# Cross-attention with 1500 keys on one core: two-chunk steps in layer 1, a third context buffer, and another order of scores, search, product and preparation on TensorE

## The chip, the cores and the metric

The kernel runs on one core of a Trainium2 chip. The metric is the device time of one execution in microseconds (us). Six engines matter here: TensorE (PE, with its weight loads PEld), VectorE (DVE), ScalarE (ACT), GpSimd (POOL), SyncE (SP, whose queue issues all DMAs of this part), and the 16 DMA engines behind that queue.

## The reference

Two decoder layers over 32 batch entries ("sequences" below) of 56 query tokens, width 128, with a context of 1500 keys each. Both layers attend to the same context, which is projected anew in each. Around them stand layer norms and two mixtures of experts, which the change leaves alone.

```python
x = x + tanh(g_xattn[0]) * diff_attention(layernorm(x), ctx)          # layer 0: 32 score heads of 4, 16 value heads of 8
x = x + tanh(g_ffn[0])   * experts0(layernorm(x))
x = x + tanh(g_xattn[1]) * masked_attention(layernorm(x), ctx, mask)  # layer 1: 16 heads of 8, mask True = hidden key
x = x + tanh(g_ffn[1])   * experts1(layernorm(x))
# attention, per sequence and head: softmax(q k^T * scale) v, with k = ctx Wk, v = ctx Wv
```

## The kernel before

`attend(T, L)` runs once for each layer, one sequence after another. The keys of a sequence are cut in 12 chunks of 125 (`NKT`, `KT`) and in 3 thirds of 500 (`TK`). One step handles one chunk.

What TensorE does in a step, with the lines of the profile:

- **scores** (L962, L968): keys times queries for the chunk, transposed, so that keys lie on partitions. Layer 0 has 1792 score columns, in two halves of 896, one for each of the two two-bank PSUM buffers `score_ps`; the parameter `place` is 0 for the first half of a step and 1 for the second. Layer 1 has 896 columns, so a step fills one buffer, and two matmuls with the mask (`mask_f`, L962) go ahead of the eight with the keys (L968). ScalarE turns each buffer into probabilities (`exps`, L1075).
- **search** (L937): the row maxima of a later sequence, found piece by piece. A piece is a matmul of 112 rows by 500 keys; VectorE reduces it (L1133 in layer 0, L1130 in layer 1, where it adds `mask_add` on the way). There are 48 pieces for a sequence in layer 0 and 24 in layer 1, issued in pairs. Three PSUM banks (`rooms`) take them in turn, so a piece waits until the piece three before it is reduced.
- **weigh**, the product (L984): probabilities of the step before times values (`vext`), accumulated in `acc_ps`. Each matmul in f32 shows as two in the trace.
- **preparation** (`use`, and `drain` on ScalarE or VectorE), placed by the table `where`: T turns the context (layer 0, L895), K and V make keys and values of a third (L904, L911), M turns the maxima (L916), F turns the output (L921) and A the normalised attention (L925). In layer 0 they use the score buffer that is free just then; in layer 1 they take a turn in the three `rooms`. `LEAD` says for which sequence: K for three ahead, V for two ahead, M for the next, F and A for the one before.

The order in a layer 0 step is: scores 0, pair 0, scores 1, first half of the product, pair 1, preparation, second half of the product. In layer 1 it is: scores, the pair, the product, preparation. The search runs five steps further ahead than the sequence (`AHEAD`): from step 7 on it works on the sequence two ahead.

What is waited for across engines, and the part of it that matters here:

- `scores` of place 0 in layer 0 waits until all exponentials of the steps before are done (`s_exp`, L953 to L955). In layer 1 it waits only for those up to the step before the last.
- Keys take a way through DRAM to be laid out anew: ScalarE drains K into `key_f`, GpSimd splits it in two halves (`split_keys`, L806, L808), SP stores both (`store_k`, L679) and reads them back with six DMAs into `kstack` (`fill_k`, L689). The first piece of a sequence waits for all six (`s_ks`).
- SP issues in order. One round of its loop is: `fill_k(n + 2)`, `load_q(n + 3)`, `next_mask(n + 3)`, `next_context(n + 4)`, `fill_m(n + 1)`, `store_k(n + 3)`. `fill_m` (L699) waits for the maxima that M has turned and VectorE has split (L1106, L1108).

## Time and profile before

| | us |
|---|---|
| median of 3 runs (2349.38 to 2350.72) | 2349.78 |
| the profiled execution | 2345.43 |
| its span, first to last instruction | 2343.1 |

| | TensorE | VectorE | ScalarE | GpSimd |
|---|---|---|---|---|
| busy us of the span | 2179.4 | 1677.4 | 1507.4 | 1278.7 |
| share | 93% | 72% | 64% | 55% |

Layer 0's attention fills the span from about 100 to 1225 us and layer 1's from about 1400 to 2165 us. Most sequences take the same time to within a few hundredths of a microsecond: 35.0 us in layer 0 and 22.3 us in layer 1. So a sequence can be read once and multiplied. A row of the timeline gives the start, the busy time, the engine and line, what is written and read, and the idle time ahead of it with what ended it. The start of the next row is what tells how long a group holds the engine, since matmuls overlap.

### The profile page before, as it was taken

Reading aid. Unit: us, or ns where it says so; the run is one execution under the profiler, and the core shown is the slowest. Engines: PE = TensorE matmul, PEld = TensorE weight load, DVE = VectorE, ACT = ScalarE, POOL = GpSimd, SP = SyncE. Lnnn points to the kernel's source line nnn. Section 1 sums busy time; section 2 is a strip of 40 time slices with the busy share of each in tenths; the row PEclk is TensorE's granted clock in tenths of the full one; section 3 lists DMA queues with packets and bytes.
Section 4 is the critical chain, followed back from the end, with each engine's and each line's share of the span. In section 5 each row is a group of like instructions: output and inputs, shape, how many; then the busy total and the mean of one; then the engine's idle time right before and its main releaser. Section 6 shows DMA issues by size and latency. Waiting matters only on the chain. (4 is left out here: it accounts for less than half of the span.)

```text
span 2343.1 us, 67447 instructions
## 1 busy us (share of the span) xinstructions
PE 2179.4 (93%) x27256; PEld 1297.5 (55%) x27256; DVE 1677.4 (72%) x3701; ACT 1507.4 (64%) x2133; POOL 1278.7 (55%) x1418
## 2 busy tenths in 40 slices
PE   3799999999999999999976967999999999999798
PEld 2255555555555555555535853666665666666576
DVE  3688888888888888888825455777776677775644
ACT  2177787787787787787773322677676667667322
POOL 5335555555655655655423445677776777772332
PEclk9599999999999999999997985999999999999799
DMA  3635344344344344344201018576665666661100
GB/s 102 130 75 117 89 100 115 89 103 114 88 103 113 94 100 111 97 98 110 48 2 64 24 35 158 126 143 148 137 140 128 136 137 138 146 124 36 55 1 16
DMA packets 95245, 227.82 MB, mean 97 GB/s; under 512 B 46308, under 2 KB 58852, under 8 KB 88292
## 3 DMA queue, kind: packets, MB, share of 16 engines
q1 hardware_dynamic: 94692, 223.67, 42.3%
q8 instruction: 210, 3.44, 0.7%
q14 instruction: 87, 0.71, 0.1%
q10 hardware_dynamic: 256, 0.00, 0.0%
HBM read 146.77 MB, written 76.48 MB: 95 GB/s over the span
## 5 line engine op out<-in xcount | busy, mean ns | idle before, releaser
L1075 ACT ACTIVATE probs<-score_ps 125x896 f32<-125x896 f32 x1152 | 1014.2, 915 | 203.3 <-PE score_ps L968 200.9
L1133 DVE TENSOR_REDUCE max_part<-max_ps 112x1 f32<-112x500 f32 x1024 | 654.3, 668 | 115.2 <-PE spare_ps L937 66.9
L984 PE MATMUL acc_ps<-probs,vext 125*32 125x224 f32 (+1 forms) x12288 | 670.7, 316 | 2.7 <-issue 2.1
L937 PE MATMUL max_ps<-kstack,qstack 48*112 48x500 f16 x1535 | 507.1, 405 | 4.7 <-DVE max_part L1133 2.6
L968 PE MATMUL score_ps<-qstack,kstack 50*125 50x224 f16 (+1 forms) x6144 | 453.6, 243 | 15.7 <-ACT probs L1075 13.9
L968 PEld LDWEIGHTS score_ps<-qstack,kstack 50*125 50x125 f16 x6144 | 343.1, 134 | 181.1 <-issue 120.2
L1130 DVE CUSTOM_DVE_ANT_0 kstack<-max_ps,kstack 112x500 f32<-112x500 f32 x511 | 335.2, 675 | 127.1 <-PE max_ps L937 75.0
L1133 DVE TENSOR_REDUCE max_part<-spare_ps 112x1 f32<-112x500 f32 x512 | 343.1, 670 | 64.3 <-PE max_ps L937 64.3
L984 PEld LDWEIGHTS acc_ps<-probs,vext 125*32 125x32 f32 x12288 | 260.8, 109 | 220.1 <-issue 151.0
L937 PE MATMUL spare_ps<-kstack,qstack 48*112 48x500 f16 x769 | 310.0, 403 | 19.2 <-issue 15.8
L937 PEld LDWEIGHTS max_ps<-kstack,qstack 48*112 48x112 f16 x1535 | 173.2, 128 | 142.7 <-issue 77.7
L806 POOL CAST khl<-kstack 128x500 f16<-128x500 f32 x189 | 112.9, 598 | 226.7 <-ACT kstack L1054 143.9
L1130 DVE CUSTOM_DVE_ANT_0 kstack<-spare_ps,kstack 112x500 f32<-112x500 f32 x257 | 173.5, 675 | 87.2 <-PE max_ps L937 75.2
L808 POOL TENSOR_TENSOR khl<-kstack,khl 128x500 f16<-128x500 f32 x189 | 201.8, 1068 | 15.3
L1459 POOL TENSOR_TENSOR kstack<-kstack,probs 112x512 f32 (+1 forms) x68 | 90.5, 1331 | 171.3 <-DVE probs L1406 171.2
L823 POOL TENSOR_TENSOR heads_out<-turned,rden 56x64 f32<-56x64 f32 x192 | 55.2, 288 | 216.9 <-DVE rden L1116 206.8
L962 PE MATMUL score_ps<-kstack 56*125 56x448 f16 x768 | 157.8, 401 | 0.2 <-issue 0.2
L777 POOL TENSOR_SCALAR kstack<-mask_in 112x1500 bf16<-112x1500 uint8 x31 | 147.1, 4746 | 2.6
L774 POOL TENSOR_SCALAR kstack<-mask_in 120x1500 f16<-120x1500 uint8 x31 | 147.6, 4762 | 0.0
L937 PEld LDWEIGHTS spare_ps<-kstack,qstack 48*112 48x112 f16 x769 | 98.7, 128 | 82.1 <-issue 60.4
L1058 ACT ACTIVATE vext<-score_ps 125x512 f32<-125x512 f32 x102 | 60.9, 597 | 76.7 <-PE score_ps L911 76.2
L766 POOL TENSOR_TENSOR qstack<-qrows,wide 112x896 f16<-112x896 f16 (+1 forms) x64 | 83.5, 1305 | 47.0 <-DMA qrows<-q_parts 24.8
(200 smaller groups left out, 2688.3 us busy)
## 6 DMA issues: line engine op xcount, KB each, us to landing
kstack<-k_parts SPq DMA_DIRECT2D x384, 187.5 KB, 6.6
k_parts<-khl SPq DMA_DIRECT2D x128, 375.0 KB, 2.7
ctx_f<-in_ctx SPq DMA_DIRECT2D x32, 750.0 KB
ctx_f<-context_parts SPq DMA_DIRECT2D x32, 750.0 KB, 4.5
context_parts<-ctx_f SPq DMA_DIRECT2D x16, 750.0 KB, 3.7
context_parts<-kstack SPq DMA_DIRECT2D x16, 750.0 KB, 3.5
mask_in<-in_mask SPq DMA_DIRECT2D x128, 82.0 KB
qrows<-q_parts SPq DMA_DIRECT2D x384, 7.0 KB, 7.0
```

The lines of the kernel that those rows point to most:

```text
L774: nc.gpsimd.tensor_scalar(by_chunk(mask_f[n % SLOTS][0:HALF + SQ, :]), turned_keys(mask_in[0:HALF + SQ, :]), -BIG, None, ALU.mult).then_in ...
L777: nc.gpsimd.tensor_scalar(by_chunk(mask_add[n % SLOTS]), turned_keys(T["mask_in2"][:, :]), -BIG * BIG, None, ALU.mult).then_inc(s_add, 1)
L806: nc.gpsimd.tensor_copy(khl[:, 0, k], key_f[:, k]).then_inc(s_kp, 1)
L808: nc.gpsimd.tensor_tensor(khl[:, 1, k], key_f[:, k], khl[:, 0, k], ALU.subtract).then_inc(s_kp, 1)
L937: nc.tensor.matmul(room(("P", n, p))[0:PIECE, 0:TK], qstack[n % SLOTS][rows, c, PIECE * i:PIECE * (i + 1)], kstack[n % SLOTS][rows, c, TK ...
L962: nc.tensor.matmul(buf[0:KT, r, 0:448], mask_f[n % SLOTS][HALF * r:HALF * r + SQ, keys], big_eye[HALF * r:HALF * r + SQ, :], start=True, s ...
L968: last = nc.tensor.matmul(buf[0:KT, r, GC * k:GC * (k + 1)], kstack[n % SLOTS][rows, h * here + k, keys], qstack[n % SLOTS][rows, h * here ...
L984: last = nc.tensor.matmul(acc_ps[32 * j:32 * j + 32, TT * S * i:TT * S * (i + 1)].rearrange("p (s c) -> p s c", s=S), vext[n % SLOTS][:, t ...
L1075: nc.scalar.activation(probs[t % 2][:, 896 * h:896 * h + 896].rearrange("k (b c) -> k b c", b=2), score_ps[(t * H + h) % 2][0:KT, :, 0:448 ...
L1130: nc.vector.tensor_tensor_reduce(masked_scores[p % 2], scores, mask_add[n % SLOTS][:, TK * third:TK * third + TK], 1.0, -3.0e38, ALU.add, ...
L1133: nc.vector.reduce_max(best, scores, AX.X).then_inc(s_red, 1)
L1459: nc.gpsimd.tensor_tensor(k, k, tmp[e % DB][:, :, :], ALU.add).then_inc(s_acc, 1)
```

## The change

1. In layer 1 a step now takes two chunks: 6 steps, four pieces each, both score buffers in each step (`place` 0 and 1). Layer 0 keeps 12 steps.
2. The order in a step is chosen by `order_of` from four, by whether this step and the one before have preparation other than A and M. The product is now undivided (16 f32 matmuls of 112 columns in layer 1, for two chunks; 8 of 224 in layer 0).
3. In layer 1 preparations move from the three `rooms` into the score buffer, as in layer 0; both transposes F of a sequence become one with four matmuls. The keys (steps 1 and 2) now stand ahead of M (step 3) and of the values (steps 3 and 4).
4. The context has a third buffer in layer 1, in the room of `XnT`. On SP, `next_context(n + 4)` now waits for the values of a sequence further back and stands behind `fill_m(n + 1)`, right ahead of `store_k(n + 3)`.
5. The additive mask is converted ahead of the other, and `next_mask` waits for both. In layer 1 the waits on `s_exp` are those of layer 0.

```diff
@@ order and places
     else:
-        where = {("V", 0): (0, 2), ("F", 0): (1, 2), ("V", 1): (2, 2), ("F", 1): (3, 2), ("V", 2): (4, 2), ("K", 0): (5, 2),
-                 ("K", 1): (6, 2), ("M", 0): (7, 2), ("K", 2): (8, 2), ("A", 0): (10, 2)}
+        where = {("F", 0): (1, 1), ("K", 0): (1, 0), ("K", 1): (2, 0), ("K", 2): (2, 1), ("M", 0): (3, 1), ("V", 0): (3, 0),
+                 ("V", 1): (4, 0), ("V", 2): (4, 1), ("A", 0): (5, 1)}
...
-    AHEAD = 5
+    AHEAD = 3 if L.masked else 5
...
+    ORDERS = {"both scores first": ("scores 0", "scores 1", "pair 0", "weigh", "pair 1", "prepare"),
+              "scores apart by a pair": ("scores 0", "pair 0", "scores 1", "weigh", "pair 1", "prepare"),
+              "scores apart by the product": ("scores 0", "pair 0", "weigh", "scores 1", "pair 1", "prepare"),
+              "pairs apart by preparation": ("scores 0", "weigh", "scores 1", "pair 0", "prepare", "pair 1")}
+
+    def order_of(n, t):
+
+        busy = [any(kind not in "AM" for kind, _, _ in at_step(*place)) for place in ((n, t), (n, t - 1) if t else (n - 1, STEPS - 1))]
+        if not busy[1]:
+            return ORDERS["both scores first"]
+        if L.masked and not busy[0]:
+            return ORDERS["scores apart by a pair"]
+        return ORDERS["pairs apart by preparation" if L.masked and busy[0] else "scores apart by the product" if busy[0] else "scores apart by the product"]
@@ SP
                 if L.masked:
-                    at_least(sp, s_v, NTHIRD * (n - 1))
+                    at_least(sp, s_v, NTHIRD * (n - 2))
...
                     next_mask(n + 3)
-                    if L.masked:
-                        next_context(n + 4)
...
                     fill_m(n + 1)
                 if n + 3 < B:
+                    if L.masked:
+                        next_context(n + 4)
                     store_k(n + 3)
@@ scores
                 number = step * 2 + place
                 h = halves_of(step)[place]
-                if L.masked:
-                    at_least(pe, s_exp, number - 1)
-                elif place == 0:
+                if place == 0:
                     at_least(pe, s_exp, number)
                 else:
                     at_least(pe, s_exp, number - 2)
```

How it moves instructions. First TensorE in layer 0, a step in which the output is turned (F, `score_ps<-wide,out_sb`) and the scores of the step behind it; before:

```order
L968 MATMUL score_ps<-qstack,kstack 125x224 x4
L937 MATMUL max_ps<-kstack,qstack 112x500 x2
L968 MATMUL score_ps<-qstack,kstack 125x224 x4
L984 MATMUL acc_ps<-probs,vext 32x224 x4
L937 MATMUL spare_ps<-kstack,qstack 112x500
L937 MATMUL max_ps<-kstack,qstack 112x500
L921 MATMUL score_ps<-wide,out_sb 56x128 x4
L984 MATMUL acc_ps<-probs,vext 32x224 x4
L968 MATMUL score_ps<-qstack,kstack 125x224 x4
```

and the same step of the change:

```order
L978 MATMUL score_ps<-qstack,kstack 125x224 x4
L949 MATMUL spare_ps<-kstack,qstack 112x500
L949 MATMUL max_ps<-kstack,qstack 112x500
L995 MATMUL acc_ps<-probs,vext 32x224 x8
L978 MATMUL score_ps<-qstack,kstack 125x224 x4
L949 MATMUL max_ps<-kstack,qstack 112x500
L949 MATMUL spare_ps<-kstack,qstack 112x500
L933 MATMUL score_ps<-wide,out_sb 56x128 x4
L978 MATMUL score_ps<-qstack,kstack 125x224 x4
```

The two halves of the product have become one, ahead of the second scores, and between the second scores and the next step's first ones only a pair and the preparation are left.

Next TensorE in layer 1 around M (`neg_max`), steps 7 and 8 before:

```order
L984 MATMUL acc_ps<-probs,vext 32x112 x8
L916 MATMUL spare_ps<-wide,neg_max 8x112
L962 MATMUL score_ps<-kstack 125x448 x2
L968 MATMUL score_ps<-qstack,kstack 125x112 x8
L937 MATMUL max_ps<-kstack,qstack 112x500 x2
L984 MATMUL acc_ps<-probs,vext 32x112 x8
L904 MATMUL spare_ps<-ctx_f,w_parts 128x500 x3
```

and step 3 of the change:

```order
L973 MATMUL score_ps<-kstack 125x448 x2
L978 MATMUL score_ps<-qstack,kstack 125x112 x8
L995 MATMUL acc_ps<-probs,vext 32x112 x16
L973 MATMUL score_ps<-kstack 125x448 x2
L978 MATMUL score_ps<-qstack,kstack 125x112 x8
L949 MATMUL max_ps<-kstack,qstack 112x500 x2
L928 MATMUL score_ps<-wide,neg_max 8x112
L923 MATMUL score_ps<-w_parts,ctx_f 125x128 x12
L949 MATMUL spare_ps<-kstack,qstack 112x500
L949 MATMUL max_ps<-kstack,qstack 112x500
```

The keys stand earlier, M has a pair ahead of it and values and a second pair behind it; VectorE reduces both pairs before it takes M.

Last SP in layer 1, one round of its loop from the masks on (`L680` and `L668` are the query rows), before:

```order
L321 DMA mask_in<-in_mask 56x1500 [waits L1_additive_mask_ready]
L323 DMA mask_in<-in_mask 56x1500
L312 DMA ctx_f<-context_parts 128x3000 [waits L1_values_ready]
L699 DMA qstack<-max_rows 1x4x112 [waits L1_max_split]
L699 DMA qstack<-max_rows 1x4x112 x3
L679 DMA k_parts<-khl 128x1500 [waits L1_key_parts_ready] x2
L689 DMA kstack<-k_parts 16x6000 [waits L1_key_part_stored0,L1_scores_ready]
L689 DMA kstack<-k_parts 16x6000 x3
```

and of the change:

```order
L323 DMA mask_in<-in_mask 56x1500 [waits L1_mask_converted,L1_additive_mask_ready]
L325 DMA mask_in<-in_mask 56x1500
L711 DMA qstack<-max_rows 1x4x112 [waits L1_max_split]
L711 DMA qstack<-max_rows 1x4x112 x3
L314 DMA ctx_f<-context_parts 128x3000 [waits L1_values_ready]
L691 DMA k_parts<-khl 128x1500 [waits L1_key_parts_ready] x2
L701 DMA kstack<-k_parts 16x6000 [waits L1_key_part_stored0,L1_scores_ready]
L701 DMA kstack<-k_parts 16x6000 x3
```

The context's load now lies between the maxima's rows and the store of the keys.

## Rows read from the trace of the kernel before

**Rows 1.** Windows: ten sequences of layer 0, eight of layer 1; busy us, clock, DMA.
```profile
437.70:787.80 350.10, 348.34 (x4030) 186.84 (x4030) 296.09 (x511) 279.33 (x382) 196.54 (x290) 1.00 0.43 102
1868.60:2047.10 178.50, 178.31 (x3099) 112.31 (x3098) 128.97 (x427) 124.89 (x177) 131.51 (x97) 1.00 0.66 139
```

**Rows 2.** Timeline of ScalarE, layer 0, two sequences' output copies and exponentials.
```profile
506.09 1.73 ACT L1075 ACTIVATE probs<-score_ps 125x896 f32<-125x896 f32 x2 [0.29 <-PE score_ps L968]
507.70 0.55 ACT L1080 ACTIVATE out_sb<-acc_ps 128x448 f32<-128x448 f32 x1
...
511.49 1.73 ACT L1075 ACTIVATE probs<-score_ps 125x896 f32<-125x896 f32 x2 [0.27 <-PE score_ps L968]
...
542.68 0.55 ACT L1080 ACTIVATE out_sb<-acc_ps 128x448 f32<-128x448 f32 x1
```

**Rows 3.** Timeline of TensorE, layer 0: end of step 0, then step 2.
```profile
506.36 0.97 PE L984 MATMUL acc_ps<-probs,vext 125*32 125x224 f32 x16
507.25 0.41 PE L937 MATMUL max_ps<-kstack,qstack 48*112 48x500 f16 x1
...
507.87 0.41 PE L968 MATMUL score_ps<-qstack,kstack 50*125 50x224 f16 x4 [0.20 <-ACT probs L1075]
...
511.04 0.41 PE L968 MATMUL score_ps<-qstack,kstack 50*125 50x224 f16 x4
511.29 0.37 PE L937 MATMUL max_ps<-kstack,qstack 48*112 48x500 f16 x1
...
511.79 0.59 PE L984 MATMUL acc_ps<-probs,vext 125*32 125x224 f32 x8
512.30 0.54 PE L937 MATMUL max_ps<-kstack,qstack 48*112 48x500 f16 x2
...
513.85 0.41 PE L968 MATMUL score_ps<-qstack,kstack 50*125 50x224 f16 x4
```

**Rows 4.** Timeline of TensorE, layer 1: a step with M, and a group V.
```profile
1970.38 0.40 PE L962 MATMUL score_ps<-kstack 56*125 56x448 f16 x2
...
1970.85 0.37 PE L937 MATMUL max_ps<-kstack,qstack 48*112 48x500 f16 x1
1971.15 0.59 PE L984 MATMUL acc_ps<-probs,vext 125*32 125x112 f32 x16
1971.67 0.26 PE L916 MATMUL max_ps<-wide,neg_max 112*8 112x112 f32 x1
```
```profile
1828.10 0.91 PE L911 MATMUL max_ps<-w_parts,ctx_f 128*125 128x128 f16 x12
```

**Rows 5.** Timeline of VectorE, layer 1: second reduction of the pair, then M.
```profile
1971.96 0.68 DVE L1130 CUSTOM_DVE_ANT_0 kstack<-max_ps,kstack 112x500 f32<-112x500 f32 x1
1972.56 0.08 DVE L1130 DVE_READ_ACCUMULATOR2_ANT max_part<- 112x1 f32 x1
1972.56 0.26 DVE L1106 TENSOR_SCALAR max_rows<-max_ps 8x112 f16<-8x112 f32 x1
1972.85 0.26 DVE L1108 SCALAR_TENSOR_TENSOR max_rows<-max_rows,max_ps 8x112 f16<-8x112 f16 x1
```

**Rows 6.** Timeline of SP's issues, layer 1, one round: keys in, maxima, keys out.
```profile
1956.06 3.71 SPq L689 DMA_DIRECT2D kstack<-k_parts  x6
```
```profile
1973.13 2.44 SPq L699 DMA_DIRECT2D qstack<-max_rows  x4
1975.78 1.47 SPq L679 DMA_DIRECT2D k_parts<-khl  x2
```

**Rows 7.** DMA issues with us to landing: 1868 to 1980, then a round's last key loads.
```profile
ctx_f<-context_parts SPq DMA_DIRECT2D x5, 750.0 KB, 4.2
k_parts<-khl SPq DMA_DIRECT2D x10, 375.0 KB, 2.6
```
```profile
kstack<-k_parts SPq DMA_DIRECT2D x2, 187.5 KB, 8.2
```

**Rows 8.** Timeline of SP's issues ahead of layer 1: context, keys out, keys in.
```profile
1409.99 0.42 SPq L312 DMA_DIRECT2D ctx_f<-context_parts  x1
1410.46 0.90 SPq L679 DMA_DIRECT2D k_parts<-khl  x2
1417.07 2.18 SPq L689 DMA_DIRECT2D kstack<-k_parts  x5
```

More of the change, by code:

```diff
@@ L63, in __init__ @@
         self.o_cols = self.cols // 4
-        self.uses_f = 2
+        self.uses_f = self.halves
+        self.steps = NKT if self.halves == 2 else NKT // 2
 L0 = Layer("L0", 32, 4, False)
@@ L257, in build @@
             T[f"{L.name}_mask_loaded"] = sem(f"{L.name}_mask_loaded")
-            T[f"{L.name}_context_loaded"] = [sem(f"{L.name}_context_loaded{i}") for i in range(1 + L.masked)]
+            T[f"{L.name}_context_loaded"] = [sem(f"{L.name}_context_loaded{i}") for i in range(3 if L.masked else 1)]
         normalise(T, "norm0", 0)
@@ L589, in attend, with at_step @@
     LEAD = {"T": 3, "K": 3, "V": 2, "M": 1, "F": -1, "A": -1}
-    def at_step(n, t, side):
-        return [(kind, n + LEAD[kind], i) for (kind, i), place in where.items()
-                if place == (t, side) and 0 <= n + LEAD[kind] < B]
+    def at_step(n, t):
+        return [(kind, n + LEAD[kind], i) for (kind, i), (step, _) in where.items()
+                if step == t and 0 <= n + LEAD[kind] < B]
     def searched(n, t, k):
-        if 2 * k >= per_step:
-            return []
-        d, place = (1, early + t * per_step) if t < NKT - AHEAD else (2, (t - NKT + AHEAD) * per_step)
+        d, place = (1, early + t * per_step) if t < STEPS - AHEAD else (2, (t - STEPS + AHEAD) * per_step)
         return [("P", n + d, place + 2 * k + r) for r in range(2)] if n + d < B else []
@@ L606, in attend @@
     for n in range(B):
-        for t in range(NKT):
-            middle, last = at_step(n, t, 1), at_step(n, t, 2)
-            spare_uses += middle + last
-            if H == 2:
-                in_scores.update({user: n * NKT + t for user in middle})
-                middle = []
-            order += searched(n, t, 0) + middle + searched(n, t, 1) + last
+        for t in range(STEPS):
+            spare_uses += at_step(n, t)
+            in_scores.update({user: n * STEPS + t for user in at_step(n, t)})
+            order += searched(n, t, 0) + searched(n, t, 1)
     order += [(kind, B - 1, i) for kind, i in turnaround]
@@ L620, in halves_of @@
     def halves_of(step):
-        return (0, 1) if step % 2 == 0 or H == 1 else (1, 0)
+        return (0, 1) if step % 2 == 0 else (1, 0)
     def room(user):
@@ L957, in scores @@
                         pe.wait_ge(s_big, n + 1)
-                buf = score_ps[(t * H + h) % 2]
-                keys = slice(KT * t, KT * t + KT)
+                buf = score_ps[h]
+                chunk, columns = (t, range(h * 2, h * 2 + 2)) if H == 2 else (2 * t + h, range(PAIRS))
+                keys = slice(KT * chunk, KT * chunk + KT)
                 if L.masked:
@@ L963, in scores @@
                                          big_eye[HALF * r:HALF * r + SQ, :], start=True, stop=False, skip_group_check=True)
-                here = PAIRS // H
-                for k in range(here):
+                for k, c in enumerate(columns):
                     for r in range(2):
                         rows = slice(HALF * r, HALF * r + KROWS + 2)
-                        last = nc.tensor.matmul(buf[0:KT, r, GC * k:GC * (k + 1)], kstack[n % SLOTS][rows, h * here + k, keys],
-                                                qstack[n % SLOTS][rows, h * here + k, :], start=not L.masked, stop=True,
+                        last = nc.tensor.matmul(buf[0:KT, r, GC * k:GC * (k + 1)], kstack[n % SLOTS][rows, c, keys],
+                                                qstack[n % SLOTS][rows, c, :], start=not L.masked, stop=True,
@@ L1164, in _ @@
             for n in range(B):
-                for t in range(NKT):
+                for t in range(STEPS):
                     for user in searched(n, t, 0):
                         reduce_piece(user)
-                    for user in at_step(n, t, 1):
-                        drain(user)
-                    if t == where["F", 1][0] + 1 and n:
+                    if t == where["F", L.uses_f - 1][0] + 1 and n:
                         reciprocals(n)
```

143 lines of the change are left out of this document (71 added, 72 removed).

## The prediction

> **What bounds the kernel now.** I read the windows first: in a stretch of ten sequences of layer 0 and of eight of layer 1, TensorE is busy for 348.3 of 350.1 us and 178.3 of 178.5 us, at granted clock 1.00, while VectorE and ScalarE are busy for 70 to 85% and GpSimd for 56 to 74% [rows 1]. So TensorE's own sequence of groups sets the pace in both layers, and the question is how long each group holds it until the next can start. Second, the timelines give the period: output copies of layer 0 are 34.98 us apart (507.70 and 542.68 in [rows 2]; the ten of [rows 1] average 35.01), and layer 1's eight take 178.5, 22.31 each [rows 1]. Third, the timeline of TensorE shows that "busy" holds slack: the product's 8 matmuls hold it for 0.51 us (511.79 to 512.30), 16 in one go for 0.89 (506.36 to 507.25) and not 1.02 [rows 3]. Each product pays about 0.13 us that does not grow with its length. Fourth, SP's issues and the landings, since a faster TensorE must find its keys there [rows 6 to 8].
>
> **Layer 0, the gain on TensorE.** The two half products become one: 1.02 becomes 0.89, and one entry into the product and one exit fall away. An entry costs 0.09: a pair of pieces of 500 columns needs 0.21 and the product behind it starts after 0.30 (1970.85 to 1971.15 in [rows 4]; layer 0 never has that neighbourhood, so I borrow it from layer 1). By TensorE alone a step would be some 0.2 shorter.
>
> **Layer 0, the wait that the order adds.** Scores 0 wait for all exponentials of the step before. Before, half a product, a pair, preparation and another half lie between scores 1 and the next scores 0: 2.35 us (511.50 to 513.85 by [rows 3], with scores 1 starting 0.46 behind scores 0). Now only the pair and the preparation do. From the start of four score matmuls to the exponential it takes 0.45 (511.04 in [rows 3], 511.49 in [rows 2]), one exponential takes 0.92 (two take 1.73), and 0.05 after its end the waiting scores start (506.09 + 1.73 = 507.82 and 507.87, the one place where they wait now). Together 1.42 from scores 1 to the next scores 0. TensorE has less to do there: scores 0.25, pair and F 1.04 (1.55 from 512.30 to 513.85, less 0.51), of which 0.13 was a wait for a room that the wider spacing removes: 1.16. So TensorE waits about 0.25 in most steps, behind which the pair, the product and everything else on its queue stand. From scores 0 to scores 1: scores 0.25, pair 0.30, product 0.89: 1.44. A step is 1.44 + 1.42 = 2.86. This step took 2.81 (511.04 to 513.85), so F and T steps lose 0.05; steps with keys or values, which are longer, gain; step 0, which has no preparation, loses most.
>
> Sum: 12 x 2.86 = 34.3. Step 1 has both scores first: there the exponentials run side by side with work and TensorE sets 2.6 (less 0.25), and the step with M and V is longer by 0.13. That is 34.2 against 35.0: 0.8 for each of 28 full sequences, **-22 us**. Ends: if the borrowed entry costs 0.2 more or the exponential is late by 0.05 in each step, 0.2 is left (-5); if steps with values keep a room wait less, 1.1 (-31). The last three sequences, with less preparation, move by under 1 us. Nothing else of layer 0 moves; VectorE's four reductions need 4 x 0.6 = 2.4 of 2.86.
>
> **Layer 1, the gain on TensorE.** Two chunks share a product: six of them save 0.13 + 0.09 each, 1.3 us; preparation between pairs also removes room waits of 0.4 to 0.8. Against it stand a wait of scores 1 in step 4 for M's drain (0.6) and a room wait of 0.4 at the pair of step 5, just behind pair 1 of step 4. TensorE alone would allow 22.3 - 1.3 - 0.8 + 1.0 = 21.2.
>
> **Layer 1, the loop of the keys.** This is what I take to set the end. The first pair of step 3 (time X) is the first of a new sequence and waits for its keys. M stands right behind it on TensorE. Follow M around:
>
> - X to M split. Before, the pair starts at 1970.85 and M is done on VectorE at 1972.85 + 0.26 = 1973.11: 2.26 [rows 4, 5]. Now VectorE takes a second pair first, which TensorE starts after the first pair (0.3), M (0.1) and V (0.91 less the 0.1 that such a group overlaps the next): 1.2 later. 3.5.
> - `fill_m` issues four DMAs, 2.44, and 0.05 to the next issue [rows 6]: 2.5.
> - The context is issued now, 0.4, and `store_k` behind it. `fill_k` may start when the first key part has landed. Alone its 375 KB land in 2.6; the context's 750 KB take 4.2 [rows 7]. Ahead of layer 1 the same three stand in a row: context issued at 1409.99, key loads at 1417.07, 7.1 later [rows 8]. For the steady loop I take the context's 4.2, plus 1.6 for 375 KB more (the difference of the two landings), less 0.15 because no mask DMAs stand right ahead of the context now: 5.65. Ends: 3.0 (0.4 + 2.6, if the store is not held up) and 7.1. I take a value near the upper end's kind, one queue, but without its delay, since the two landings come from the steady loop itself.
> - `fill_k`: first issue 1956.06, the last two issues end at 1959.77 and land 8.2 after theirs [rows 6, 7], about 1967.3: 11.2.
>
> Then X comes again for the next sequence: 3.5 + 2.5 + 5.65 + 11.2 = **22.8**. Before, the same round was 2.3 + 2.5 + 0.2 + 2.6 + 11.2 = 18.8, with 3.5 to spare. So the keys' loop becomes longer than TensorE's 21.2 and even than the old period: +0.5 for each of 28 sequences, **+14 us**. With 3.0 the loop is 20.2 and TensorE's 21.2 holds; with 7.1 it is 24.3.
>
> The Trainium skill, DMA: Bandwidth & Descriptors, section on queues, rings and completion order, says that on each DMA engine the descriptors of one queue are consumed in ring order, while nothing orders completion across the 16 engines. By that rule the store stands behind all of the context on every engine and waits for the slowest; the trace agrees ahead of layer 1, with 7.1 in place of 3.0 [rows 8]. The same page fits 2.0 us plus the bytes at 436 GB/s to a DMA; an estimate by it for the context and the first part, 1.15 MB, is 4.6; the loop would be 21.8, a gain of 14 us where I forecast a loss of 14. No run here shows that sum yet; the 4.2 of the context alone is 0.5 above what it gives for 0.77 MB.
>
> The third buffer itself brings nothing: no row shows TensorE waiting for a context inside the loop. GpSimd needs some 17 us of a sequence (131.5 / 8 = 16.4 busy [rows 1]) and its last split comes ahead of `store_k`'s new place, so I cost the turned mask order at 0. The last two sequences, with less search, are paced by the exponentials, +1.
>
> **The time.** Against the profiled execution (2345.4, of which 2343.1 is span): 2345.4 - 22 + 14 = 2337.4. It lies 4.4 below the median of the runs; against that median 2349.8 - 8 = **2342**.
>
> **Rivals.**
> 1. The DMAs hold each other up little: the loop is 20.2, TensorE sets 21.2, -31 in layer 1: 2349.8 - 22 - 31 = 2297. For it: the queue is idle ahead of the context's new place. Against it: [rows 8]. Chance 0.14. (The fit of the Trainium skill's DMA page lies halfway, at 2314.)
> 2. Slower: the store behind the context is as late as ahead of layer 1. It outweighs layer 0 from a gap of 5.9 between context and key loads (22.3 + 22/28 = 23.1 for the loop); at 7.1 the loop is 24.3, +55: 2383. For it: the one place that shows this row of DMAs shows this. Against it: there the queue had other loads ahead of it, and the context alone took longer. Chance 0.20.
> 3. Layer 0 gains nothing, since the exponentials come later than in the rows or the product's entry costs more: 2349.8 + 14 = 2364. Against it: each term but one stands in a row of layer 0. Chance 0.12.
> 4. TensorE's wait at step 3, 1.6 us in each sequence, lowers its granted clock, which is 1.00 now [rows 1]. Then X to M takes 1 us more, the loop 23.8: 2369. Chance 0.04.
>
> My forecast has 0.50, with its own range 2326 to 2358 (the layer 0 term within 9 of -22, the gap from 5.2 to 6.1).
>
> **How the numbers follow.** Two kernels closer than 0.2% (4.7 us) can't be told apart here. Faster: 0.34 of the 0.50, and rival 1: 0.48. Same: 0.11 of the forecast and 0.05 of rivals 2 and 3: 0.16. Slower: the rest, 0.36. The range 2300 to 2374 takes in the forecast, rivals 3 and 4, the near sides of 1 and 2, and leaves out some 0.2.
>
> **What would show it.** In layer 0: output copies 34.2 apart; scores 0 waiting for the exponentials by about 0.25 in most steps and 0.9 at step 1; the product's 16 in 0.89. In layer 1: copies 22.8 apart; TensorE idle for about 1.6 us ahead of the first pair of step 3, the keys landing last; `fill_k` issued 5.6 after the context. It is wrong if layer 1's period is 21.2 with no such wait, if the fill comes long after the keys are stored, or if layer 0 waits for something but the exponentials.

## The result, and the profile after

The changed kernel takes 2388.03 us (median of 3 runs, 2386.75 to 2392.78) against 2349.78: the ratio is 1.0167, 95% interval 1.0144 to 1.0190. It is slower by 38 us, where 8 us faster was forecast. Its profiled execution took 2386.75, of which 2385.0 is span, at a mean granted clock of 0.93.

The windows of ten sequences of layer 0 and of eight of layer 1 answer to [rows 1] (stretch; length, then busy us of PE, PEld, DVE, ACT and POOL with instructions, granted clock, DMA share, GB/s):

```profile
501.96:843.04 341.08, 321.93 (x4030) 169.09 (x4030) 305.87 (x512) 278.69 (x381) 196.88 (x290) 1.00 0.44 104
1684.19:1880.51 196.32, 176.49 (x3098) 129.48 (x3096) 127.52 (x425) 125.05 (x169) 129.85 (x97) 0.93 0.67 129
```

Layer 0 is shorter: 34.11 us a sequence instead of 35.01. Layer 1 is longer: 24.5 in these eight instead of 22.3, with TensorE idle for 20 of 196 us and its clock at 0.93. Over the whole of layer 1, first to last output copy, it is 743.1 against 682.7 us. From the profiled runs the bill is this: layer 1 begins 18.9 us earlier (its first output copy at 1462.9 instead of 1481.8) and takes 60.4 longer, which gives the 41 to 42 between the two executions and spans.

TensorE's waits in layer 1 (1480 to 2100) name the cause (us in total, times, longest); the kernel before has no such line among its waits:

```profile
PE max_ps L949 <- DMA kstack<-k_parts: 53.1, 24, 4.0
PE acc_ps L995 <- issue: 6.7, 7, 1.8
```

One round in the timelines of TensorE, VectorE and SP, answering to [rows 4 to 6 and 8]:

```profile
1868.26 0.42 PE L949 MATMUL max_ps<-kstack,qstack 48*112 48x500 f16 x2 [2.37 <-DMA kstack<-k_parts]
1868.60 0.26 PE L928 MATMUL score_ps<-wide,neg_max 112*8 112x112 f32 x1
...
1869.61 0.66 PE L949 MATMUL spare_ps<-kstack,qstack 48*112 48x500 f16 x1
...
1870.99 1.72 PE L995 MATMUL acc_ps<-probs,vext 125*32 125x112 f32 x32
```
```profile
1870.91 0.67 DVE L1136 CUSTOM_DVE_ANT_0 kstack<-max_ps,kstack 112x500 f32<-112x500 f32 x1
1871.51 0.08 DVE L1136 DVE_READ_ACCUMULATOR2_ANT max_part<- 112x1 f32 x1
1871.51 0.26 DVE L1112 TENSOR_SCALAR max_rows<-score_ps 8x112 f16<-8x112 f32 x1
1871.80 0.26 DVE L1114 SCALAR_TENSOR_TENSOR max_rows<-max_rows,score_ps 8x112 f16<-8x112 f16 x1
```
```profile
1872.09 2.46 SPq L711 DMA_DIRECT2D qstack<-max_rows  x4
1874.60 0.44 SPq L314 DMA_DIRECT2D ctx_f<-context_parts  x1
1875.09 0.89 SPq L691 DMA_DIRECT2D k_parts<-khl  x2
1881.66 2.67 SPq L701 DMA_DIRECT2D kstack<-k_parts  x6
```
```profile
1892.88 0.42 PE L949 MATMUL max_ps<-kstack,qstack 48*112 48x500 f16 x2 [2.63 <-DMA kstack<-k_parts]
```

This is the loop of the prediction, term by term: X at 1868.26, M split at 1872.06 (3.8), M's rows and the context issued (2.5), key loads 7.06 behind the context's issue, next X 11.2 behind the first of these; 24.6 in all. Over 28 rounds the same four terms are 3.87, 2.5, 7.09 and 11.2 on the mean, 24.7 in all. The DMA issues (KB each, median us to landing) show which transfers became slower; [rows 7] had 4.2 and 2.6. First the context, from the page, then the store in five sequences of layer 1 (1503 to 1630; the page's own figure for the store mixes both layers):

```profile
ctx_f<-context_parts SPq DMA_DIRECT2D x22, 750.0 KB, 5.6
XnT<-context_parts SPq DMA_DIRECT2D x10, 750.0 KB, 5.8
```
```profile
k_parts<-khl SPq DMA_DIRECT2D x12, 375.0 KB, 6.7
```

And the windows of the same round, the first from X to just after M's split, the second the rest up to the next wait's end:

```profile
1868.26:1872.80 4.54, 4.54 (x61) 3.43 (x63) 3.00 (x10) 1.51 (x2) 1.81 (x3) 0.62 0.20 42
1872.90:1892.80 19.90, 17.20 (x328) 12.45 (x324) 12.98 (x43) 14.12 (x19) 14.58 (x11) 1.00 0.80 149
```

Right behind its wait of 2.37 us TensorE runs part of the time at the lower clock of 1.2 GHz: the product's 32 matmuls take 1.72 there and 0.97 elsewhere.

### The profile page after: what moved, and what is told of

Its sections match the earlier page's. It is cut to its first block and busy times, and to the rows that moved or that the text cites. A ratio compares the mean times of both kernels' runs of the same rounds, so it can differ in the third digit from the quotient of the medians.

```text
span 2385.0 us, 67374 instructions
## 1 busy us (share of the span) xinstructions
PE 2087.1 (88%) x27256; PEld 1305.6 (55%) x27256; DVE 1701.8 (71%) x3701; ACT 1505.0 (63%) x2101; POOL 1273.8 (53%) x1418
## 5 line engine op out<-in xcount | busy, mean ns | idle before, releaser
L1081 ACT ACTIVATE probs<-score_ps 125x896 f32<-125x896 f32 x1152 | 1041.3, 916 | 325.9 <-PE score_ps L978 318.6
L1139 DVE TENSOR_REDUCE max_part<-max_ps 112x1 f32<-112x500 f32 x1024 | 663.8, 672 | 83.7 <-PE max_ps L949 43.5
L995 PE MATMUL acc_ps<-probs,vext 125*32 125x224 f32 (+1 forms) x12288 | 577.7, 318 | 10.2 <-issue 8.1
L949 PE MATMUL max_ps<-kstack,qstack 48*112 48x500 f16 x1536 | 472.9, 404 | 69.9 <-DMA kstack<-k_parts 59.5
L978 PE MATMUL score_ps<-qstack,kstack 50*125 50x224 f16 (+1 forms) x6144 | 468.6, 253 | 72.5 <-ACT probs L1081 66.8
L978 PEld LDWEIGHTS score_ps<-qstack,kstack 50*125 50x125 f16 x6144 | 321.1, 137 | 319.7 <-ACT probs L1081 246.1
L995 PEld LDWEIGHTS acc_ps<-probs,vext 125*32 125x32 f32 x12288 | 314.3, 112 | 181.7 <-issue 122.5
L949 PEld LDWEIGHTS max_ps<-kstack,qstack 48*112 48x112 f16 x1536 | 153.2, 130 | 135.0 <-DMA kstack<-k_parts 63.2
L1062 ACT ACTIVATE vext<-score_ps 125x512 f32<-125x512 f32 x192 | 114.7, 597 | 135.9 <-PE score_ps L923 122.8
```

Of the source, the lines that this page charges most:

```text
L949: nc.tensor.matmul(room(("P", n, p))[0:PIECE, 0:TK], qstack[n % SLOTS][rows, c, PIECE * i:PIECE * (i + 1)], kstack[n % SLOTS][rows, c, TK ...
L978: last = nc.tensor.matmul(buf[0:KT, r, GC * k:GC * (k + 1)], kstack[n % SLOTS][rows, c, keys], qstack[n % SLOTS][rows, c, :], start=not L. ...
L995: last = nc.tensor.matmul(acc_ps[32 * j:32 * j + 32, TT * S * i:TT * S * (i + 1)].rearrange("p (s c) -> p s c", s=S), vext[n % SLOTS][:, c ...
L1062: nc.scalar.activation(vext[n % SLOTS][:, THIRD * i:THIRD * i + THIRD, :, :].rearrange("k t u (a e) -> k t (u a) e", a=2)[:, :, :, 0:VD], ...
L1081: nc.scalar.activation(probs[t % 2][:, 896 * h:896 * h + 896].rearrange("k (b c) -> k b c", b=2), score_ps[h][0:KT, :, 0:448], ACT.Exp, sc ...
L1139: nc.vector.reduce_max(best, scores, AX.X).then_inc(s_red, 1)
```

## Experiments

The theory: in layer 1 a chain of DMAs, from M's rows over the store of the keys to the key loads, closes on itself through the wait at the fourth step (step 3), and is longer than TensorE's own work because the context load stands in it. The rivals: the new step order costs TensorE the time itself; or the DMA engines' throughput sets the period. "L1 period" below is the median distance of two output copies of layer 1 in the profiled run: 22.3 before, 24.6 after. The means are higher, 22.6 and 24.8, since some sequences take longer than the rest. Ratios are to the kernel before.

**e1: the context load back to its old place.**

```diff
                     next_mask(n + 3)
+                    if L.masked:
+                        next_context(n + 4)
 ...
                 if n + 3 < B:
-                    if L.masked:
-                        next_context(n + 4)
                     store_k(n + 3)
```

> The kernel after, with one edit: in layer 1 the context load goes back to where it was issued before the change, right behind the masks and ahead of the rows of M, so that between M's rows and the store of the keys' parts nothing stands on SP's queue. Theory A (the loop of the keys through DRAM sets the period of layer 1, and the context load in it is what made it long): from the store's issue to the first key load 2.6 us as in the kernel before instead of 6.6, the sum of the loop 3.5 + 2.5 + 0.5 + 2.6 + 11.2 = 20.3, which is under TensorE's own 21.2 a sequence, so TensorE sets the period again: 24.8 becomes 21.2 to 21.5, the whole 2388 - 28 x 3.4 = 2293 (2285 to 2305), and TensorE's wait for keys at the fourth step is gone. Theory B (the new order of layer 1's steps costs TensorE the time, by waits between short pieces and a lower clock, and the keys are only late because of it): the period stays near 24.8 and the whole at 2375 to 2390. Theory C (the context load is slow wherever it stands and takes the engines from the key loads): period 23 to 24, whole 2340 to 2365.

2298.69 us, ratio 0.9762 (0.9722 to 0.9802), L1 period 21.00. Theory A. One round of SP, and TensorE's waits over eight sequences:

```profile
1574.11 0.37 SPq L314 DMA_DIRECT2D ctx_f<-context_parts  x1
1578.52 2.44 SPq L711 DMA_DIRECT2D qstack<-max_rows  x4
1581.00 0.92 SPq L691 DMA_DIRECT2D k_parts<-khl  x2
1583.84 4.08 SPq L701 DMA_DIRECT2D kstack<-k_parts  x6
```
```profile
PE score_ps L973 <- ACT probs L1081: 4.6, 8, 0.6
PE max_ps L949 <- DVE max_part L1136: 1.2, 8, 0.2
```

The key loads go out 2.84 us behind the store instead of 6.57, and no wait for keys is left in these sequences (one of 0.9 us in the whole layer). What remains is 0.6 at the fifth step's scores 1 (step 4) and 0.15 at a room of the sixth step's pair (step 5), the two places that the prediction counted against layer 1's TensorE time. The profile puts the first down to ScalarE; but ScalarE's last exponential ended 0.5 ahead (1578.08), M's split on VectorE ended at 1578.50, and the scores start at 1578.60, so it is M's drain. So both parts of the change can be had, and this version beats both kernels. It is the best of the study.

**e2: the store ahead of the context, the context ahead of the key loads.**

```diff
-                    if L.masked:
-                        next_context(n + 4)
                     store_k(n + 3)
+                    if L.masked:
+                        next_context(n + 4)
```

> The kernel after, with one edit: the store of the keys' parts is issued ahead of the context load in layer 1, the context load still ahead of the next key loads. It tells a shared queue in order from shared engines. Theory A1 (a queue's transfers are served in order of issue): the store lands in 2.6 us, but the key loads behind it stand behind the context's 4.5 us, so their landing is as late as before: period 24 to 25, whole 2370 to 2390. Theory A2 (only a transfer that waits for its data to land pays; loads behind a load share the engines and the key loads' 11.2 us are set by their own count and latency): period 21.2 to 22, whole 2290 to 2310. Theory B (layer 1's new step order itself): 2375 to 2390 with no change in TensorE's wait pattern.

2337.54 us, ratio 0.9944 (0.9918 to 0.9971), L1 period 22.4: between the theories. The store lands in 3.1, and the key loads' last landing comes 11.9 behind their first issue instead of 11.2, so a load ahead of loads costs them only 0.7. But the context now takes 8.2 us and is waited for itself:

```profile
PE score_ps L916 <- DMA ctx_f<-context_parts: 15.9, 14, 3.7
PE score_ps L916 <- DMA XnT<-context_parts: 10.7, 8, 1.7
```

A new wait in the place of the old one; neither theory had it.

**e3: the kernel before with only the context load moved down.**

```diff
                     next_mask(n + 3)
-                    if L.masked:
-                        next_context(n + 4)
 ...
                 if n + 3 < B:
+                    if L.masked:
+                        next_context(n + 4)
                     store_k(n + 3)
```

> The kernel before, with only one edit: in layer 1 the context load is issued where the changed kernel issues it, behind the rows of M and right ahead of the store of the keys' parts (two context buffers, old steps, old layer 0). Theory A: the loop there is 2.26 + 2.5 + 0.5 + 6.6 + 11.2 = 23.1 a sequence against the 22.3 that TensorE needs, so the period becomes 23.1 and up to 24 if TensorE's clock falls behind its wait: whole 2350 + 28 x 0.8 = 2372 (2365 to 2390), with a wait for keys at TensorE that the kernel before doesn't have. Theory B (the new step order costs the time): this edit is hidden, 2350 (2348 to 2353). Theory C (the context load is as harmless here as its 2.7 us shows): the gap grows to 5.65 only, loop 22.1, whole 2350 to 2355.

2372.92 us, ratio 1.0078 (1.0055 to 1.0102), L1 period 23.1. Theory A's numbers: the key loads are issued 6.5 behind the store, and TensorE has the wait that the kernel before lacks:

```profile
PE max_ps L937 <- DMA kstack<-k_parts: 8.1, 10, 1.8
PE spare_ps L937 <- DMA kstack<-k_parts: 3.9, 5, 1.4
```

The place of one DMA costs the old kernel 0.8% by itself, with its old steps. The step order isn't what lost the time.

**e4: M ahead of the pair that waits for the keys, context still late.**

```diff
                         elif work in ("pair 0", "pair 1"):
+                            if L.masked and work == "pair 0":
+                                for user in at_step(n, t):
+                                    if user[0] == "M":
+                                        use(user)
                             search(searched(n, t, int(work[-1])))
...
```

(left out here: M's old place is skipped, and on VectorE M's drain goes ahead of that pair's reductions)

> The kernel after, with the context load left ahead of the store, but M of the next sequence transposed by TensorE ahead of the first pair of the fourth step (the pair that waits for the keys) instead of behind it, and drained by VectorE ahead of that pair's reductions. Theory A: M no longer waits for the keys, so the chain M, rows of M, context, store, key loads runs a sequence ahead: about 1.0 + 2.5 + 0.5 + 6.6 + 11.2 = 21.8 from M's transposition to the next pair, against 21.2 of TensorE; the wait and the loop share the difference and the period is 21.3 to 21.8: whole 2388 - 28 x 3.2 = 2298 (2288 to 2315), with the gap still at 7. Theory B (step order or clock, not the loop): 2375 to 2390. Theory C (the engines of the DMA are the limit: bytes a sequence): period 24 or more whatever the order.

2314.55 us, ratio 0.9846 (0.9801 to 0.9891), L1 period 21.3. The gap is hardly shorter (6.1 behind the store), but the loop is opened, since M no longer waits behind X on TensorE. The wait for keys is 4.9 us in all instead of 53.1. The total lies 17 above the expected 2298: a dozen sequences took 21.8 to 25.9 us, and TensorE has 14 us of waits for "issue" there, single ones up to 2.3 us (more on these at the end).

**e5: half the context's bytes.**

```diff
-        sp.dma_start(context_parts(T, n % 3), T["ctx_dram"][n:n + 1, :, :, :]...
+        parts = slice(0, 2) if n < 4 else slice(0, 1)
+        sp.dma_start(context_parts(T, n % 3)[:, parts, :], T["ctx_dram"][n:n + 1, :, parts, :]...
```

> The kernel after with the context load in its late place, but from the fifth context on it brings only the high parts (375 KB instead of 750); the low parts of an older context stay in the buffer, so the output is not the reference's, and all other work is unchanged. It asks whether the gap between the store and the next key loads (6.6 us with the whole context ahead, 2.9 with none) grows with the bytes ahead or is a fixed price of a load ahead of a store. Theory D (bytes: the store waits behind the context's packets on each engine): gap 2.9 + 3.7 / 2 = 4.8, loop 24.35 - 1.8 = 22.5 plus the half clock's share, total 2388 - 28 x 1.9 = 2335 (2325 to 2345). Theory E (fixed, whatever the size): gap 6 to 6.6, total 2375 to 2388. Theory F (the load is slow only from a certain size): gap 3 to 3.5, TensorE's 21.0 to 21.3 sets the period, total 2292 to 2300.

The gap behind the store is 4.7 (expected 4.8), the L1 period 22.45 (22.5). One round; its key loads went out at 1852.08:

```profile
1846.48 0.44 SPq L315 DMA_DIRECT2D ctx_f<-context_parts  x1
1846.97 0.90 SPq L692 DMA_DIRECT2D k_parts<-khl  x2
```

So with 0, 375 and 750 KB ahead of it the store's first part frees the key loads after 2.9, 4.7 and 6.6 us: 1.85 us for each 375 KB, a price by bytes and not a fixed one. The total, 2348.1 us (ratio 0.9976, 0.9961 to 0.9991), is 13 above the expected 2335, by a dozen sequences of 23 to 27 us among which the "issue" waits are again (18 us, single ones up to 3.2).

**e6: the wait filled with work.** Ten products right ahead of X, and nothing else:

```diff
+                            if L.masked and t == 3 and work == "pair 0" and n + 3 < B:
+                                v, c = ("V", n + LEAD["V"], 0), n + LEAD["K"]
+                                pe.wait_ge(s_exp, in_scores[v] * 2 + 1)
+                                for k in range(10):
+                                    nc.tensor.matmul(room(v)[:, 0:TK], Wk[0], ctxT[c % CTX][:, k % 2, 0:TK],
+                                                     start=True, stop=True, skip_group_check=True)
                             search(searched(n, t, int(work[-1])))
```

> The kernel after, context in its late place, with 10 extra products of 500 columns by TensorE (2.1 us, into a bank that the next group overwrites) right ahead of the pair that waits for the keys in layer 1. They lie where TensorE waits 2.1 us a sequence on the mean. It prices the half clock that follows that wait. Theory G (the wait lets the clock fall, and that costs 0.5 us a sequence: the stretch from the pair to M's rows takes 4.2 to 4.6 us in half the rounds instead of 3.5): granted clock 1.00 in layer 1, the loop 3.5 + 2.5 + 0.5 + 6.6 + 11.2 = 24.3 every time, total 2388 - 28 x 0.45 = 2375 (2370 to 2380). Theory H (the half clock falls in the slack and costs nothing): 2388, or a little more, since where the keys come earlier than the extra products end they delay the pair: 2386 to 2396. If the extra products delay the pair on the mean, the period is above 24.8.

The windows of five sequences each show the clock, here two of this run and one of the changed kernel:

```profile
1505.00:1630.00 125.00, 115.53 (x1977) 80.60 (x1981) 78.73 (x263) 77.77 (x105) 81.02 (x60) 0.99 0.66 125
1757.00:1879.00 122.00, 113.66 (x1993) 79.88 (x1985) 79.43 (x266) 78.08 (x106) 81.06 (x60) 1.00 0.68 129
```
```profile
1626.00:1751.00 125.00, 107.66 (x1913) 78.64 (x1915) 79.41 (x264) 77.99 (x105) 81.20 (x60) 0.95 0.67 125
```

It stays at 0.99 to 1.00, and X to M's split is 3.50 in every round, where the changed kernel has 3.8 to 4.6 in 12 of 28 (3.87 on the mean). So the clock falls behind the wait, and with it goes 0.4 us of the loop. The median L1 period is 24.3 as expected. But the whole of layer 1 is no shorter in the profiled runs, 742.7 us against 743.1: in three rounds, of 26.9 to 28.1 us, the keys had landed 1.8 to 4.4 us before TensorE, which had "issue" waits on the way, reached the pair. The total is 2383.74, ratio 1.0131 (1.0111 to 1.0151): 4 to 8 us below the changed kernel, but the intervals overlap. What the clock costs the whole kernel is not shown.

**e7: e1 with another order in layer 0.**

```diff
-        ... else "scores apart by the product" if busy[0] else "scores apart by the product"]
+        ... else "scores apart by a pair"]
```

> The version with the context load ahead of M's rows (2299 us), with one edit in layer 0: there the order of a step is scores, pair, scores, product, pair, preparation, with the product still in one piece, instead of scores, pair, product, scores, pair, preparation. It asks which part of layer 0's change brings its 0.9 us a sequence (35.01 to 34.11). Theory I (the rows before: an undivided product alone saves 0.13 + 0.09 a step of TensorE's time, but scores 1 then wait 0.3 for the drain of the step before's preparation, which stands in the bank they write): 35.1 a sequence, total 2299 + 31 x 1.0 = 2330 (2320 to 2336). Theory J (TensorE's own time is all that counts, so the undivided product brings the gain in any order): 34.1 or less, total 2290 to 2302.

2372.38 us, ratio 1.0092 (1.0071 to 1.0113). Layer 0 takes 36.71 us a sequence, not 35.1 (theory I) and not 34.1 (theory J). A step and the start of the next on TensorE, then ScalarE's drains of the preparations ahead of both steps:

```profile
538.26 0.41 PE L978 MATMUL score_ps<-qstack,kstack 50*125 50x224 f16 x4
538.50 0.37 PE L949 MATMUL max_ps<-kstack,qstack 48*112 48x500 f16 x1
538.55 0.41 PE L949 MATMUL spare_ps<-kstack,qstack 48*112 48x500 f16 x1
539.10 0.41 PE L978 MATMUL score_ps<-qstack,kstack 50*125 50x224 f16 x4
539.44 0.96 PE L995 MATMUL acc_ps<-probs,vext 125*32 125x224 f32 x16
540.33 0.42 PE L949 MATMUL max_ps<-kstack,qstack 48*112 48x500 f16 x2
...
542.09 0.41 PE L978 MATMUL score_ps<-qstack,kstack 50*125 50x224 f16 x4 [0.16 <-ACT kstack L1053]
```
```profile
538.37 0.59 ACT L1071 ACTIVATE turned<-score_ps 56x512 f32<-56x512 f32 x1 [0.76 <-PE score_ps L933]
...
541.36 0.59 ACT L1053 ACTIVATE kstack<-score_ps 128x500 f32<-128x500 f32 x1 [0.80 <-PE score_ps L907]
```

The pair holds TensorE for 0.60 (538.50 to 539.10), where it takes 0.21 in the kernel before. The second scores write the bank in which the last preparation stands, and the program makes them wait for its drain. They start 0.14 behind its end (538.96, then 541.95), and so it is in all 179 such places between 300 and 900 us. The profile books 0.16 us of this as idle time ahead of 542.09, and nothing ahead of 539.10. In the kernel before half a product lies between the preparation and the next scores, and the drain has mostly ended 0.27 before the second scores start. So the mechanism is theory I's, at 0.39 a step instead of 0.3. An estimate from these rows: 11 steps of 0.39 make 4.3, less 12 times 0.22 for the undivided product leaves 1.7, and measured is 36.71 less 35.01. By this the undivided product is worth the 0.2 a step that the prediction gave it; a run with the halves in the new order, which would show it, was not made. Shown is that the gain is lost, and more, where the drain falls ahead of the second scores.

**e8: e1 and e4 together.**

> Both edits that each took the keys' loop off the end: the context load ahead of M's rows, and M transposed and drained ahead of the first pair of the fourth step. Theory A: keys are never waited for; what M first adds over the context edit alone is that scores 1 of the fifth step no longer wait for M's drain: the steady period of layer 1 is 20.75 (the shortest of the M-first run) instead of 21.00, total 2299 - 28 x 0.25 = 2292 (2286 to 2299). Theory B' (something else of layer 1 waits for the keys or the context): no shorter than 2299.

2306.35 us, ratio 0.9803 (0.9784 to 0.9822): no gain over e1. The expected 20.75 is there in nine sequences, and no wait for keys or for M's drain is left, but the other nineteen take 21 to 26.7, with 19 us of "issue" waits among them.

**e9: the masks directly ahead of the late context.** The call `next_mask(n + 3)` moves from behind `load_q` to just ahead of `next_context(n + 4)`.

> The kernel after with the four mask loads of layer 1 moved down, from ahead of M's rows to directly ahead of the late context load, where the kernel before had them (there the context landed in 4.5 us, in the changed kernel in 5.6 to 5.8). It asks why the context takes longer in its late place, which is the part of the gap that the forecast left out. Theory K (what stands directly ahead on the queue decides: behind other loads the context lands in 4.2 to 4.6): the context's landing falls to 4.3 to 4.6, the first key load is issued 5.4 to 5.6 us behind the store instead of 6.6, and since the masks add 1.7 to 1.8 us of issuing the loop is 24.35 + 1.8 - 1.1 = 25.1, total 2388 + 28 x 0.4 = 2399 (2392 to 2408). Theory L (the context is slow because the store stands behind it on the same queue and both are served together): landing stays 5.4 to 5.8, loop 26.2, total 2388 + 28 x 1.4 = 2427 (2418 to 2436).

2462.03 us, ratio 1.0472 (1.0447 to 1.0498), L1 period 27.2. The DMA issues of its page:

```profile
ctx_f<-context_parts SPq DMA_DIRECT2D x22, 750.0 KB, 5.6
XnT<-context_parts SPq DMA_DIRECT2D x10, 750.0 KB, 5.9
```

Theory L: what stands ahead of the context doesn't matter, what is issued behind it does. With a store 0.5 us behind it the context lands in 5.3 to 5.9 (after, e3, e4, e9, e10); with no store behind it for 2.9 us or more it lands in 4.3 to 4.6 (before, e1, e8, e11). The period is 1.0 longer than that theory gave, since the longer wait (90.7 us in all, up to 5.2) is followed by the lower clock in 27 rounds of 28: X to M's split is 4.4 to 4.6 in each.

**e10: only M's drain earlier on VectorE.**

```diff
-                    for user in searched(n, t, 1):
-                        reduce_piece(user)
                     for user in at_step(n, t):
                         drain(user)
+                    for user in searched(n, t, 1):
+                        reduce_piece(user)
```

> The kernel after, with one edit on VectorE alone: M is drained between the reductions of the fourth step's two pairs instead of behind both. TensorE's order, the context's late place and all DMAs stay. It prices the first term of the keys' loop. Theory A (the loop through DRAM sets the period, and each of its terms counts in full): from the first pair to M's rows 2.3 us instead of 3.5 to 4.6, loop 24.35 - 1.2 = 23.15 and less of a penalty from the low clock, total 2388 - 28 x 1.3 = 2352 (2342 to 2360). Theory M (the DMA engines' throughput a sequence, not the chain, sets 24.8): no change, 2385 to 2390.

2349.47 us, ratio 0.9992 (0.9977 to 1.0007), L1 period 23.25 (expected 23.15). One round on VectorE, with X at 1850.39:

```profile
1851.54 0.68 DVE L1136 CUSTOM_DVE_ANT_0 kstack<-max_ps,kstack 112x500 f32<-112x500 f32 x1
1852.14 0.26 DVE L1112 TENSOR_SCALAR max_rows<-score_ps 8x112 f16<-8x112 f32 x1
1852.43 0.26 DVE L1114 SCALAR_TENSOR_TENSOR max_rows<-max_rows,score_ps 8x112 f16<-8x112 f16 x1
1852.80 0.68 DVE L1136 CUSTOM_DVE_ANT_0 kstack<-spare_ps,kstack 112x500 f32<-112x500 f32 x1
```

X to M is 2.3 in most rounds, with the gap still at 6.6. Two instructions of 0.26 us, moved past two reductions, are worth 38 us. The term became 1.5 shorter on the mean and the round 1.2: it counts in full wherever the keys come last, and in four rounds near 1640 to 1730 they did not. The DMAs are the same and the period is shorter, so the throughput of the DMA engines is not the limit.

**e11: e1 with two context buffers.** The load waits for `NTHIRD * (n - 1)` V groups instead of `(n - 2)`, and `n % 3` becomes `n % 2`.

> The version with the context load ahead of M's rows (2299 us), with the third context buffer taken away again: two buffers, and the load waits for the third V group of the sequence whose context it replaces, in the fifth step, with M's rows and the store behind it on SP's queue. It tests the sentence of the prediction that the third buffer itself brings nothing. Theory N (it is the buffer that lets the context stand ahead of M's rows at all in the new step order): from the first pair to V's last drain 6.6 us, then the context's issue 0.45, M's rows 2.5, the store, and key loads 7.1 behind the context's issue at the earliest: loop 6.6 + 7.1 + 11.2 = 24.9, total 2385 to 2400. Theory O (the buffer brings nothing, the place of the load does): 2294 to 2305.

2409.82 us, ratio 1.0251 (1.0226 to 1.0277), L1 period 25.2. Theory N in its direction: without the buffer the old place can't be had with the new steps. Its chain was another. SP waits for the third V group, so M's rows go out 3.5 us late, and in this layout it is the next sequence's first scores that wait for them, as the program has it; the keys come in time:

```profile
PE score_ps L973 <- issue: 56.4, 24, 3.0
PE max_ps L949 <- DMA kstack<-k_parts: 1.6, 4, 0.5
```

The profile books it as "issue". By the timelines the rows are issued at 1867.00 to 1869.44, and the scores start at 1871.20 behind 2.00 us of idle time:

```profile
1867.00 2.44 SPq L711 DMA_DIRECT2D qstack<-max_rows  x4
```
```profile
1871.20 0.64 PE L973 MATMUL score_ps<-kstack 56*125 56x448 f16 x2 [2.00 <-issue]
```

All 24 of these waits end 1.5 to 2.8 us behind the issue of the rows.

## Why the prediction was wrong

- **Layer 0, right.** Forecast 34.2 a sequence, measured 34.11. Scores 0 wait for the exponentials by 0.22 to 0.25 in four steps of a sequence, by 0.06 in three and by 0.80 at step 1 (forecast: about 0.25 in most steps, 0.9 at step 1). Layer 1 begins 19 us earlier (forecast 22); 28 sequences give 25, of which 3 go at the start of layer 0 and 3 at its end and behind it. Rival 3 fell. What the working leaves out is a second wait, of scores 1 for the drain of the preparation in their bank. In the order of the change it costs nothing; in that of e7 it costs more than the undivided product brings.
- **Layer 1, TensorE's own time, right.** 21.2 forecast, 21.00 in e1, with the two counted waits where they were said to be (0.6 as forecast, and 0.15 booked where 0.4 was forecast).
- **The loop of the keys, right as a mechanism.** It was named with its four terms, and three of them had the forecast size: 3.5 for X to M (at full clock), 2.5 and 11.2, with X 0.04 behind the last landing. e3, e4 and e10 each changed one link and moved the period by what the sum says.
- **The term that failed: the gap between the context's issue and the first key load,** forecast 5.65, measured 7.1 on the mean (0.5 and 6.6). The prediction had the right value in [rows 8] and set it aside "since the two landings come from the steady loop itself". But the context's 4.2 there was the landing of a load with no store behind it for 6.6 us or more. With the store half a microsecond behind it, it lands in 5.6 (e9), and the store 1.5 later. The correction by the masks, 0.15, was of no use. The gap of rival 2, held at 0.20, was the true one: 1.45 us in each sequence, 41 us in 28.
- **The clock, rival 4, at 0.04, came true beside it.** Its condition was a wait of 1.6 us; the wait became 2.2 on the mean of the 24 that the profile books, and the lower clock after it adds 0.4 to the loop (3.87 for X to M instead of 3.5; forecast was 1 us more in every round). The two rivals are one case: a longer gap makes the wait longer, and the wait makes the loop longer again. The sum 22.85 + 1.45 + 0.35 is the 24.7 that a round takes on the mean. Holding them as separate cases with separate chances was the second mistake: rival 2 alone gave 2383, while a loop of 24.8 against the 22.6 that the kernel before takes on the mean gives 2349.8 - 22 + 28 x 2.2 = 2389, and the range ended at 2374, below both. That 22.6 is a small miss of its own: the prediction took 22.3 for every sequence, but five of the kernel before take 22.7 to 25.8, 8 us in all.
- **The skill's estimate.** By the fit in the Trainium skill, DMA: Bandwidth & Descriptors, section Anatomy of one DMA, the gap was 4.6. The page gives that fit for a single DMA issued from GpSimd; here two are issued from SP. The measured gap is 7.1 for the same 1.15 MB, and 5.2 with half the context, where the fit gives 3.8. The ring-order rule of its section on queues, rings and completion order fits e1 and e5, where the store lands later with every 375 KB right ahead of it. In e9 four mask loads of 82 KB, issued 0.4 to 1.7 us ahead of the context, add nothing to the gap (7.1 again).
- **"The third buffer itself brings nothing" was wrong as a sentence.** No context was waited for, as said, but e11 shows that the buffer is the condition for the good place of the load. The prediction compared the change only with the kernel before and never asked what the same parts in another order would give; that was 89 us of difference.

## What to carry to other kernels

A wait deep in a pipeline may be part of a loop that leaves the chip's engines and comes back through DRAM. Add up such a loop term by term, including how many instructions an engine does between the wait and the result that starts the next transfer; e10 shows that two small instructions in it can be worth 38 us. Keep large loads with time to spare out of the stretch between a result and the store that needs to leave at once: the same load ahead of four small DMAs instead of behind them, on the same queue, made 3.7% here. And when a profile has one place where the same DMAs stand in the same row, take its time over a sum of landings measured apart.

## What the runs showed of the hardware

- A load's time to landing depends on what is issued behind it: the context's 750 KB took 4.3 to 4.6 us with no store behind it for 2.9 us or more, 5.3 to 5.9 with a 375 KB store issued 0.5 us behind, and 8.2 to 8.9 with a store just ahead and six key loads following (e2).
- Behind TensorE's waits for keys the stretch from X to M's split ran at 1.2 GHz for all or part of it in 21 rounds of 28 in the changed kernel (waits of 1.0 to 4.0 us, 2.4 on the mean) and in 27 of 28 in e9 (waits of 2.7 to 5.9), though the DMA engines were busy. With the wait filled by products whose results are not read the clock stayed at 0.99 to 1.00 (e6).
- TensorE's waits for "issue", in which nothing that the page shows was late, add up to 4 us over layer 1 before, 8 after, 14 in e1, 18 in e5 and 19 in e8, single ones of up to 3.2 us. In e1 they lie near 1640 to 1740 and 1900 to 2080. The traces point at their cause. Two DMA queues are named "instruction" in the profile, and on the first, q8, 79 transfers of 16 KB run in layer 1 of the changed kernel (1480 to 2110; transfers, MB, share of the engines):

```profile
q8 instruction: 79, 1.29, 1.0%
```

  Of all such waits in layer 1 longer than 0.3 us (110 in the twelve traces without e11, most of whose waits are those for M's rows), every one ended 1.2 to 1.9 us behind the end of a transfer on q8; a moment taken at random lies so in one case of ten. In e1 such a transfer ran from 1725.23 to 1726.82, and the longest wait but one, of 2.2 us, ended at 1728.14. So TensorE most likely waited for its own instructions. That is read from the times alone: no run changed these transfers, and why they come late in some stretches is open.
- An estimate: without these waits and what follows them e1 would have 28 sequences of 21.0 us in layer 1, where it has 606 us: some 18 us less.
